# Reading back the second half of an expert layer beside the keys of the next layer, and relation products in two sweeps

## The reference

```python
out = x + gate0 * y[expert0] + gate1 * y[expert1]      # per node, 256 features
```

```python
h = layernorm(x)                                       # per node
k = elu(h @ Wk) + 1                                    # keys of a linear attention; context = k.T @ h
w[r] = sum over b of comp[r, b] * basis[b]             # 16 relation matrices from 8 bases, each 256 x 256
y[n, r] = h[n] @ w[r]                                  # every node times every relation matrix
```

## Time and profile before

| what | value |
|---|---|
| median of the timed runs | 6538.76 us |
| the profiled execution | 6526.06 us, span 6524.2 us |
| PE busy | 4982.3 us (76%) |
| DVE busy | 4132.2 us (63%) |
| POOL busy | 3750.0 us (57%) |
| last tile of the experts ends | 3078 us from the span's start |
| keys begin and end | 3153 and 3311 us |
| products end, next stage's first gather | 3994 and 4000 us |

### The profile page before, as it was taken

How to read it: one execution, slowest core, us unless ns; L and a number is a source line. 1 busy time by engine, 2 the same in 40 slices (tenths; PEclk the granted TensorE clock), 3 DMA queues, 4 the chain that set the end, 5 groups by cost and what they waited for, 6 DMA issues and landing times. The chain is left out here.

```text
span 6524.2 us, 104936 instructions
## 1 busy us (share of the span) xinstructions
PE 4982.3 (76%) x26438; PEld 3596.9 (55%) x26691; DVE 4132.2 (63%) x9549; ACT 1517.9 (23%) x3021; POOL 3750.0 (57%) x3893
## 2 busy tenths in 40 slices
PE   6867777777777775898499997777777777766694
PEld 4535555555555554897344444655555555555583
DVE  5338999888888887334640002877777777666454
ACT  1213333333333333454123331000000000000341
POOL 4457777777777773403510003777777777777524
PEclk8979999888898986899899998888888888888597
DMA  4323444444444444323224443333333333333345
GB/s 152 113 77 109 112 112 112 112 112 112 112 112 112 112 111 139 112 81 99 78 110 162 164 162 132 109 109 108 108 108 109 108 109 108 106 104 102 121 151 152
DMA packets 360162, 755.97 MB, mean 116 GB/s; under 512 B 91218, under 2 KB 225264, under 8 KB 347184
## 3 DMA queue, kind: packets, MB, share of 16 engines
q0 software_dynamic: 175104, 491.59, 26.3%
q1 hardware_dynamic: 177856, 256.44, 11.3%
q10 hardware_dynamic: 7056, 6.43, 0.3%
HBM read 556.32 MB, written 199.66 MB: 116 GB/s over the span
## 5 line engine op out<-in xcount | busy, mean ns | idle before, releaser
L868 POOL DMA_INDIRECT rg_ring<-y_dram,src_at x1612 | 1537.7, 954 | 1191.7 <-POOLq L906 700.7
L868 POOL DMA_INDIRECT ga_ring<-h_dram,src_at x1612 | 1544.9, 958 | 507.0 <-issue 457.0
L1622 PE MATMUL rg_psS<-rg_ring,rg_hot_w 128*128 x4000 | 1153.5, 453 | 401.6 <-SPq L844 315.8
L1622 PEld LDWEIGHTS rg_psS<-rg_ring,rg_hot_w 128*128 128x128 f32 x4000 | 906.0, 231 | 645.7 <-issue 481.9
L1042 PE MATMUL ga_psS<-ga_msg,ga_hot 128*128 128x280 f32 x4000 | 1198.4, 456 | 43.6 <-DVE ga_msg L1182 37.0
L1042 PEld LDWEIGHTS ga_psS<-ga_msg,ga_hot 128*128 128x128 f32 x4000 | 853.6, 221 | 312.0 <-DVE ga_msg L1182 87.5
L1739 DVE TENSOR_SCALAR rg_hot_t<-rg_psB,pair_node,place 128x1024 bf16<-128x1024 f32 x253 | 338.6, 1338 | 615.8 <-PE rg_psB L915 615.8
L1431 PE MATMUL rr_psY<-rr_wr,rr_xt 128*128 128x512 f32 x1568 | 675.9, 594 | 2.4 <-DMA rr_xt<-x_dram 2.4
L1182 DVE SCALAR_TENSOR_TENSOR ga_msg<-ga_psW,ga_ring 128x2112 f32<-128x2112 f32 x251 | 587.3, 2340 | 0.0
L1431 PEld LDWEIGHTS rr_psY<-rr_wr,rr_xt 128*128 128x128 f32 x1568 | 298.6, 191 | 377.8 <-issue 374.5
L2026 POOL DMA_INDIRECT f_row<-yg_dram,f_pos_y x196 | 196.0, 1000 | 490.4 <-issue 268.8
(11 more groups left out here) (391 smaller groups left out, 6819.1 us busy)
## 6 DMA issues: line engine op xcount, KB each, us to landing
y_dram<-rr_big SPq DMA_DIRECT2D x98, 1024.0 KB, 3.9
f_x<-xg_dram SPq DMA_DIRECT2D x224, 128.0 KB
yg_dram<-f_work SPq DMA_DIRECT2D x224, 128.0 KB
ga_ring<-h_dram,src_at POOLq DMA_INDIRECT x1612
rg_ring<-y_dram,src_at POOLq DMA_INDIRECT x1612
f_w<-L_ffn_W SPq DMA_DIRECT2D x16, 512.0 KB, 6.1
h_dram<-op_row SPq DMA_DIRECT2D x49, 136.0 KB, 1.8
xt_dram<-op_xt SPq DMA_DIRECT2D x49, 128.0 KB, 1.8
```

The source lines that it names most:

```text
L868: p.indirect_dma_start(ring[:, (g % R) * G + j, :], None, table, bass.IndirectOffsetOnAxis(ap=rows[:, g * G + j:g * G + j + 1], axis=0)).t ...
L1622: o = pe.matmul(psS[:, u % 2, 0:C], hot_w[:, u % 2, j, :], rows[:, j, :], start=j == 0, stop=j == G - 1)
```

## The change

The second half's read-back leaves `experts`. The gates, the row numbers `pos_y` and the measures `six` are kept for the next stage, and the separate statistics stage of this place goes.

In the keys stage POOL now gathers the 23 blocks of the second half, two gathers each, into eight slots of the products' store buffer. The bases have a buffer of their own. DVE mixes block 26+i after the keys of block i+3. The statistics come in three spans: blocks 0 to 25 at the start, 26 to 37 at block 14, 38 to 48 at block 25. The staging of a block moves from POOL to ACT, as an activation with scale and bias. DVE forms only the first eight relation matrices (64 of the 128 `weigh`) in this stage, from block 23 on.

The products run in two sweeps over the 49 blocks: relations 0 to 7, then 8 to 15. Each visit is four chunks, one load of the transposed rows and one store of 1024 KB. DVE forms the other eight matrices beside the first sweep, and PE waits for them (`formed`) before the second.

```diff
-def relation_rows(nc, z, k, S, late):
+def relation_rows(nc, z, k, S, late, six, gate, pos_y):
...
-    YP = REL * C // 512
+    YP = REL * C // 1024
+    HALF_R = REL // 2
+    SLOTS = 8
+    LATE = 3
+    FORM = 23
+    mid = (half + NB + 1) // 2
+    spans = [(0, half), (half, mid), (mid, NB)]
+    stats_at = {mid - half - 1 + LATE: 1, NB - half - 1 + LATE: 2}
...
             def _(p):
-                start_at(p, BASE, staged)
-                p.wait_ge(ready, 1)
-
-                for b in range(NB):
-                    p.wait_ge(summed, done(b - 4))
-                    p.tensor_scalar(st[:, b % 4, 0:C], k.xb[:, b * XW:b * XW + C], k.mean[:, b:b + 1],
-                                    k.rstd[:, b:b + 1], ALU.subtract, ALU.mult).then_inc(staged, 1)
+                for i in range(NB - half):
+                    if i >= SLOTS:
+                        p.wait_ge(mixed, i - SLOTS + 1)
+                    for r in range(2):
+                        p.indirect_dma_start(back_y[:, i % SLOTS, r, :], None, k.yg_dram[1],
+                                             bass.IndirectOffsetOnAxis(ap=pos_y[:, r, half + i:half + i + 1], axis=0)
+                                             ).then_inc(y_in[i % SLOTS], 16)
 
             @block.scalar
...
+                def stage(b):
+                    for s, (lo, _) in enumerate(spans):
+                        if b == lo:
+                            act.wait_ge(measured, s + 1)
+                    if b >= 4:
+                        act.wait_ge(summed, done(b - 4))
+                    act.activation(st[:, b % 4, 0:C], k.xb[:, b * XW:b * XW + C], ACT.Identity, bias=shift[:, b:b + 1],
+                                   scale=k.rstd[:, b:b + 1]).then_inc(staged, 1)
...
+                for b in range(NB):
+                    if b + 2 < NB:
+                        turn(b + 2)
+                    if b + 1 < NB:
+                        raise_up(b + 1)
+                    if b + 4 < NB:
+                        stage(b + 4)
+                    if b in stats_at:
+                        root_of(stats_at[b])
...
+                def mix(i):
+                    b = half + i
+                    mine = k.xb[:, b * XW:b * XW + C]
+                    v.wait_ge(y_in[i % SLOTS], 32 * (i // SLOTS + 1))
+                    v.scalar_tensor_tensor(mine, back_y[:, i % SLOTS, 0, :], gate[:, 0, b:b + 1], mine, ALU.mult, ALU.add)
+                    v.drain()
+                    v.scalar_tensor_tensor(mine, back_y[:, i % SLOTS, 1, :], gate[:, 1, b:b + 1], mine, ALU.mult, ALU.add
+                                           ).then_inc(mixed, 1)
+                    v.drain()
+                    v.bn_stats(six[:].rearrange("p b s -> p (b s)")[:, b * 6:(b + 1) * 6], mine)
+
+                def formed(b):
+                    return HALF_R * nb * max(b - FORM + 1, 0) // (NB - FORM)
                 floor(0)
                 for b in range(NB):
                     keep(b)
                     if b + 1 < NB:
                         floor(b + 1)
-                    if b == 1:
+                    if b - 1 in stats_at:
+                        scales(stats_at[b - 1])
+                    if 0 <= b - LATE < NB - half:
+                        mix(b - LATE)
+                    if b in stats_at:
+                        spreads(stats_at[b])
+                    if b == FORM:
                         v.wait_ge(of_basis, 16 * (nb + 1))
-                        v.drain()
-                    for n in range(done_of(b - 1), done_of(b)):
-                        weigh(n)
+                    for n in range(formed(b - 1), formed(b)):
+                        weigh(v, n)
...
-                def body(b, u, i):
-                    pe.wait_ge(placed[u], i * 16 + 16)
+                def visit(n, u, part):
+                    pe.wait_ge(placed[u], (n - u) * 8 + 16)
                     for q in range(YP):
 
-                        pe.wait_ge(parts_in, b * YP + q + 1)
+                        pe.wait_ge(parts_in, n * YP + q + 1)
                         for kc in range(KC):
                             t = pe.matmul(psY[:, q % 2, :], xt[:, u, kc * P:(kc + 1) * P],
-                                          wr[:, kc, q * 512:(q + 1) * 512], start=kc == 0, stop=kc == KC - 1)
+                                          wr[:, kc, (part * YP + q) * 512:(part * YP + q + 1) * 512], start=kc == 0,
+                                          stop=kc == KC - 1)
                         t.then_inc(parts, 1)
                     pe.sem_inc(freed, 1)
...
+                in_twos(pe, 4, NB, lambda n, u: visit(n, u, 0))
+                pe.wait_ge(formed, 1)
+                in_twos(pe, NB, 2 * NB, lambda n, u: visit(n, u, 1))
...
                 v.tensor_copy(late.ctxw[:], psC[:, :, 0:C])
+                for n in range(HALF_R * nb, REL * nb):
+                    o = weigh(v, n)
+                o.then_inc(formed, 1)
...
+                def place(n, u, part):
+                    sp.wait_ge(freed, done(n - 2))
+                    sp.dma_start(xt[:, u, :], k.x_dram[ds((n - part * NB) * P, P), :]).then_inc(placed[u], 16)
+
+                def visit(n, u, part, following=None):
+                    if following is not None:
+                        place(n + 1, 1 - u, following)
+                    sp.wait_ge(parts_in, n * YP + YP + 2)
+                    sp.dma_start(rows[ds((n - part * NB) * P, P), part * width:(part + 1) * width], y[:, u, :]
+                                 ).then_inc(stored[u], 16)
...
+                if kept is not None:
+                    for u in range(2):
+                        sp.wait_ge(y_out[u], 16 * below(NT, u))
...
+                    if h == 1 and kept is not None:
+                        break
...
-                in_fours(v, half, NB, mix)
+                if kept is None:
+                    in_fours(v, half, NB, mix)
...
-            normalise_stats(nc, "n4", k.xb, mean, rstd, 1e-5, NB, width=XW, six=six)
```

More of the change, by code:

```diff
@@ L1210, with in_twos @@
     pass
-def relation_rows(nc, z, k, S, late):
+def in_twos(eng, lo, hi, body):
+    first, last = lo + lo % 2, hi // 2 * 2
+    for n in range(lo, first):
+        body(n, n % 2)
+    with eng.Fori(first // 2, last // 2) as i:
+        body(i * 2, 0)
+        body(i * 2 + 1, 1)
+    for n in range(last, hi):
+        body(n, n % 2)
+def relation_rows(nc, z, k, S, late, six, gate, pos_y):
     NB = z.NB
+    half = z.HALF_NB
     nb = S["L1_gnn_basis"].shape[0]
-    YP = REL * C // 512
+    YP = REL * C // 1024
[6 more added lines that the diff above has]
+    stats_at = {mid - half - 1 + LATE: 1, NB - half - 1 + LATE: 2}
     with ExitStack() as c:
@@ L1247, in relation_rows @@
                              "floored", "powered", "kept_keys", "summed"))
+        mixed, var_ready, root_ready, measured = (sem(x) for x in ("mixed", "var_ready", "root_ready", "measured"))
+        y_in = [sem(f"y_in{u}") for u in range(SLOTS)]
         saved = [sem("saved0"), sem("saved1")]
```

163 lines of the change are left out of this document (91 added, 72 removed).

## The result

The changed kernel takes 6433.39 us (median of 4 runs, 6432.53 to 6435.64) against 6536.71 us of the kernel before: a ratio of 0.9842, 95% interval 0.9825 to 0.9859. Its profiled execution took 6432.53 us (span 6430.7).

The account below looks back on a forecast made before the run. Three limits were named: POOL's gathers at the experts' end, DVE in the keys, PE in the products. 64.4 us from the read-back plus 0.6 from the keys made 65 less: 6474 us on the runs' scale, range 6456 to 6500.

Parts of the forecast that it names:

- the change part by part: Step pricing read-back, keys and products in turn against the profiled 6526.06 us; total 65 us less.
- The 6.9 us between the two ... stay: Experts' end, between last mix and statistics: all engines meet and semaphores are cleared; 6.9 us kept.
- 62.3 + 2.4: Experts' end: read-back (62.3 us) and separate statistics stage (2.4 us) go; keys begin 64.4 us earlier after 0.3 off.
- the sum of 158.0: Keys stage rebuilt from DVE's order with mixes and statistics in, 64 weighs out: 158.0 us against 158.6 before.
- blocks 3 to 22 with one lot of statistics: Keys: 20 blocks of keep, floor and mix at 2.40 us, 48.0, plus 3.3 for one later statistics span.
- DVE remains the limit, narrowly: Keys, mixing blocks: DVE needs 2.40 us a block, PE at most 2.33.
- the 0.50 from floor to what follows: Keys, DVE: 0.50 us from floor to the next instruction, part of the 2.40 us per mixing block.
- a later span of statistics: Keys: each of two later spans adds short DVE instructions and a root on ACT with table loads; 3.3 us each.
- The 3 us taken for the collision of loads and gathers: Keys' beginning: 16 gathers (2 MB) beside 3.6 MB of loads; between nothing and 6.6 us, 3 taken.
- the rival's price: Products, late loads: landing over about 5.2 us after issue stops PE every visit, 96 us per us beyond; chance 0.05.
- The rival of keys that don't absorb the mixes: Keys: ACT's stage enters the chain or gathers set the pace; +23 to +29 us, about 6500; chance 0.20.
- Full blocking between mixes and gathers: Keys: both gathers of a block stand in line with DVE's mix for 23 blocks; +44 us, 6518; chance 0.02.

## Why the prediction was wrong

In the three stages that the change touches, the direction and most of the mechanism were right (65 us predicted, 77 measured). The time still fell 23 us below the range, for three reasons, the first of which is a step that the sum did not have at all.

**Gathers elsewhere, the largest part: -22 us where nothing was counted.** The step that failed is the change part by part itself: it priced the three stages that it touches and took the others as unchanged. Taking the stagings off POOL makes the 3224 gathers of attend and relations some 7 ns faster each in the mean. The run with the staging on ACT alone shows it (25 us in those two stages), and 49 small tensor-scalars bring it back. Why it is so stays open. Without these 22 us the time would have been about 6455, at the very edge of the range. In the profile of before one thing was to be seen, but it does not explain the step: the same kind of gather took 946 ns in the earlier trace rows and 957 in the attend stage.

**"The 6.9 us between the two ... stay": -6.8 us.** The prediction took them for the meeting of all engines and the clearing of semaphores. They belong to POOL's end, 10.3 us after its last gather, of which the last mix hid 3.4. With POOL's last gather 70 us earlier they are hidden. The other part of that stretch, 62.3 + 2.4, came as predicted.

**The keys: -7.1 us against the sum of 158.0; it was 150.9 in the first profile of after (151.7 in the second).** By its terms: beginning 19.2 (18.5 predicted; +0.7); keep 1 to keep 3, 6.1 (5.7; +0.4); blocks 3 to 22 with one lot of statistics 47.2 (48.0 + 3.3; -4.1); blocks 23 to 25 with the other 13.2 (12.6 + 3.3; -2.7); the rest 65.2 (63.3 + 3.3; -1.4). "DVE remains the limit, narrowly" was wrong for the mixing blocks: in every second one DVE's floor waits for PE. The mis-sized terms are two. The mixing block takes 2.27 us in the mean: the 0.50 from floor to what follows was read at a weigh, which has a drain ahead of it; a mix has none there and follows after 0.34. And a later span of statistics costs about 1.3 us, not 3.3: in the block of the first one keep to keep took 3.23 us instead of 2.27, the next 2.57; DVE waits for the root on ACT nowhere: it hides beside the mix.

The 3 us taken for the collision of loads and gathers came out near: 10.0 us of waiting instead of 7.1, with the DMA engines busy 0.92 instead of 0.66. No run took the gathers away from these loads, so that the gathers cause it is argued. The products cost nothing, as predicted: loads land in 3.8 us in the median and 4.1 at most, and PE waits for none but the first. But the rival's price was too high: a visit that starts late also ends late, and the load for the visit behind it can then be there in time. With two slots and four sweeps a load was 1.6 + 2.7 - 3.43 = 0.9 us late. At every one of 196 visits that would be 171 us, at every second one 85, and 114 were measured: in the trace 132 of the 195 steps from one visit's first matmul to the next are over 0.3 us longer than 3.43, in long stretches every second one, in others several in a row. The 114 us are two thirds of 171, so by this one run each us of lateness would cost two sweeps some 65 us (an estimate), not 96.

The rival of keys that don't absorb the mixes fell: DVE's keeps wait for ACT 11.4 us in all, 10.0 of them in the block of the third turn. Full blocking between mixes and gathers fell as well:

```profile
L1320 POOL DMA_INDIRECT rr_y<-yg_dram,pos_y x46: 941/947/1179, 3074.7 to 3139.4; - x46
...
L1467 DVE SCALAR_TENSOR_TENSOR xb<-rr_y,gate,xb 128x256 f32<-128x256 f32 x23 | 11.1, 484 | 1.7
L1465 DVE SCALAR_TENSOR_TENSOR xb<-rr_y,gate,xb 128x256 f32<-128x256 f32 x23 | 10.9, 474 | 0.0
```

28 of these 46 gathers run at the same time as an instruction of a mix; their median is 947 ns, as that of the other 18. The mixes' two instructions took 474 and 484 ns in the mean, where the earlier trace rows had 0.48 us for the first, with 1.7 us of idle time before them in all. By the Trainium skill (SBUF — State Buffer, Who interferes with whom) a DVE instruction with two SBUF inputs contends with a GpSimd instruction that reads SBUF, for an exclusive lock. Between these mixes and these gathers no such blocking shows; whether the rule means a gather at all, no run here tells.

## What to carry to other kernels

When two stages are bound by different engines, moving work between them pays about the exposed time of the one, if the other still fits its own limit; look also at what the next stage's first wait is, since here reordering its loads gave another 14 us. With two slots a prefetch needs a visit longer than issue plus landing (5.4 us under a visit of 6.9 cost nothing here, 4.3 under 3.43 cost 114 us); otherwise it needs more slots. And compare the untouched stages of both profiles first: a fifth of this gain lay there.

## What was not expected of the hardware

- A gather of the attend stage on POOL (128 rows) took 946 or 947 ns in the median in programs with 82 or 83 tensor-scalars on POOL and 957 in programs with 131, though the 49 further ones stand 700 us behind the stage. Programs with 107 (960) and with none (949) fit, if the 3 ns of the slower chip are taken off. 49 memsets or 98 idle instructions did nothing, and with 131 the gathers of the second half of the first layer's experts still took 946. Why stays open.
- A stage whose last POOL instruction is a gather was followed by the next stage 10.3 us after that gather in three kernels, with or without a loop on DVE; 12.3 us in one where POOL waited for the landing.
- A load of 128 KB issued right behind a store landed in 3.8 us in the median behind 1024 KB (after, 98 loads) and in 2.7 behind 512 KB (four sweeps, 196 loads, with two slots and with four).
